# Column-group products, levels by halves and a fourth round: one large change to a three-stage audio kernel on TensorE

## What is computed

```python
h = einsum('bfh,kh->bfk', frames, D)                # DCT
# attention block, on layernorm(h)
q, k = exp(rmsnorm(xq @ Wq.T)), exp(rmsnorm(xk @ Wk.T));  v = xv_ @ Wv.T;  g = sigmoid(xg @ Wg.T)
A = lam * A + k v^T ;  z = lam * z + k              # per head, step by step over the frames
att = g * (q^T A) / (q . z) @ Wo.T
x = x + att
x = x + gelu(layernorm(x) @ W1.T) @ W2.T
h = h + x
# expert block, on layernorm(h)
x_attn = normed @ attn_w.T + attn_b + xf
y = gelu(x_attn @ fc1_w[e].T + fc1_b[e]) @ fc2_w[e].T + fc2_b[e]
h = h + gelu(y @ next_w.T + next_b)
```

## Time and profile before

| | us |
|---|---|
| median of 3 runs | 1223.17 |
| lowest and highest | 1221.0 and 1224.21 |
| the profiled execution | 1218.9 |
| its span, first to last instruction | 1217.1 |
| TensorE busy in it | 1138.9 (94%) |
| VectorE busy | 986.5 (81%) |
| ScalarE busy | 621.5 (51%) |
| GpSimd busy | 300.9 (25%) |

### The profile page before, as it was taken

How to read it: one execution, slowest core, us unless ns; L and a number is a source line. 1 busy time by engine, 2 the same in 40 slices (tenths; PEclk the granted TensorE clock), 3 DMA queues, 4 the chain that set the end, 5 groups by cost and what they waited for, 6 DMA issues and landing times.

```text
span 1217.1 us, 43497 instructions
## 1 busy us (share of the span) xinstructions
PE 1138.9 (94%) x17955; PEld 807.8 (66%) x17955; DVE 986.5 (81%) x3362; ACT 621.5 (51%) x1100; POOL 300.9 (25%) x174
## 2 busy tenths in 40 slices
PE   4799999999999999999999999999999999999997
PEld 4576676666767676766666667666676766667664
DVE  7878788797887979788796887979879797987962
ACT  3346446363554736446363554736446364554634
POOL 4123131221403223131311403223131221403211
PEclk8799999999999999999999999999999999999999
DMA  5321313222141312313222141312313222141210
GB/s 188 106 64 39 113 43 110 65 79 56 43 132 44 87 47 66 110 43 113 63 78 55 44 130 46 88 45 63 112 44 110 63 80 57 43 132 45 87 55 17
DMA packets 51492, 91.48 MB, mean 75 GB/s; under 512 B 9536, under 2 KB 26592, under 8 KB 51296
## 3 DMA queue, kind: packets, MB, share of 16 engines
q1 hardware_dynamic: 51296, 88.69, 24.1%
HBM read 19.50 MB, written 9.78 MB: 24 GB/s over the span
## 4 chain that ended last, share of the span: by engine, by line
PE 83%; DVE 9%; POOL 4%; issue 3%; ACT 2%; DVEq 0%; POOLq 0%
PE bank L1056 10%; PE bank L1049 9%; PE bank L1084 9%; PE bank L1078 8%; PE bank L919 8%; PE bank L914 7%; PE bank L1014 7%; PE bank L998 5%; PE bank L990 4%; PE bank L1033 4%; POOL nrm L391 3%; PE bank L1029 3%; PE bank L954 3%; PE bank L943 2%; PE bank L994 2%
## 5 line engine op out<-in xcount | busy, mean ns | idle before, releaser
L514 ACT ACTIVATE px<-bank 128x512 f32<-128x512 f32 (+1 forms) x128 | 72.8, 569 | 218.0 <-PE bank L998 152.9
L763 DVE COPY_PREDICATED px<-mask,bank 128x512 f32<-128x512 uint32 (+1 forms) x128 | 88.6, 692 | 79.6 <-issue 76.8
L1078 PE MATMUL bank<-xa,f1w 128*128 128x512 f32 (+1 forms) x256 | 124.7, 587 | 14.8 <-DVE qtok L704 13.0
L1056 PE MATMUL bank<-w,hid 128*128 128x128 f32 x1024 | 121.9, 277 | 17.2 <-ACT hid L533 17.2
L1056 PEld LDWEIGHTS bank<-w,hid 128*128 128x128 f32 x1024 | 116.7, 192 | 31.6 <-ACT hid L533 31.6
L1014 PEld LDWEIGHTS bank<-qx,ki 128*32 128x32 f32 x7680 | 89.6, 110 | 42.3 <-issue 33.9
L827 DVE TENSOR_TENSOR ki<-k,rp 128x96 f32<-128x96 f32 (+13 forms) x512 | 113.2, 295 | 0.6 <-ACT k L499 0.6
L397 POOL TENSOR_TENSOR ab<-af,heads 128x896 f32<-128x896 f32 x16 | 40.8, 2552 | 291.1 <-DVE af L755 291.1
L1049 PE MATMUL bank<-c,w 128*128 128x512 f32 (+1 forms) x256 | 111.4, 568 | 1.1 <-ACT c L527 0.9
L1084 PE MATMUL bank<-hid,f2w 128*128 128x512 f32 (+1 forms) x256 | 107.5, 563 | 0.0
L1014 PE MATMUL bank<-qx,ki 128*32 128x16 f32 x7680 | 99.2, 193 | 6.9 <-issue 6.6
(11 more groups left out here) (142 smaller groups left out, 2414.0 us busy)
## 6 DMA issues: line engine op xcount, KB each, us to landing
qx<-qq SPq DMA_DIRECT2D x256, 96.0 KB
hs<-hs SPq DMA_DIRECT2D x32, 532.0 KB, 4.4
v<-v_f SPq DMA_DIRECT2D x16, 512.0 KB, 3.9
gz<-gate_f SPq DMA_DIRECT2D x16, 512.0 KB, 4.7
xT<-in_xT SPq DMA_DIRECT2D x16, 468.5 KB, 4.0
f1w<-in_fc1T SPq DMA_DIRECT2D x16, 256.0 KB, 2.7
f2w<-g_dram SPq DMA_DIRECT2D x16, 256.0 KB, 3.0
out<-t_sum SPq DMA_DIRECT2D x16, 256.0 KB, 2.7
```

The costliest lines, as they stand in the source:

```text
L763: V.copy_predicated(px[c % 2][0:n, :, 0:n], mask[0:n, 0:n].rearrange("p (o m) -> p o m", o=1).to_broadcast([n, HEADS, n]), bank[DIAG][0:n, ...
L1056: last = mm(dst[:, P * i:P * i + P], hid[:, j, P * m:P * m + P], w2[:, j, :], start=(j == 0), stop=(j == 3))
L1078: mm(dst[:, 0:width[g]], f1w[:, P * j:P * j + P], xa[:, cols(g)], start=True, stop=True).then_inc(f1_ok, 1)
```

## The change

- **Products round the columns.** In `pairs_a` the 64-column product is two of 32 columns and comes first, then the two of L994, then the twelve of L990 with the window as the inner loop.
- **States by heads.** The state product of `scan` is four, one for each head's 32 columns.
- **Levels by halves.** `inside`, `between` and `qlev` run twice a batch on 512 frames. `ki`, `ko`, `kw` now hold one half; the second half's wait (`last_pairs`) is for `pairs_b(3)` of the same batch, the first half's for `pairs_b(7)` of the batch before.
- **The second norm on ScalarE.** `normed2` becomes one small VectorE instruction a half (`offset2`) and eight ACTIVATE a batch.
- **Fewer buffers cleared.** `qc` and `qq` no longer; of others only the frames beyond 938; `ki`, `ko`, `kw` just ahead of their first use in `inside` and `between` of batch 0. The first DMA of samples no longer waits for a clear.
- **Its own order.** LAST is 3, so 19 rounds. The DCT and the first transposes are stage 0; q, k, v up to `scan(3)`, `pairs_a(4)` and `attends(0)` stage 1; `pairs_b(4)` to the first half of the expert stage 2; the rest stage 3. Every engine's order and the bank table are new.

```diff
-LAST = 2
+LAST = 3
@@ def last_pairs
+        def last_pairs(eng, b, g):
+            if g:
+                eng.wait_ge(pb_ok, nth(b, TILES, TILES // 2))
+            else:
+                before(eng, pb_ok, b, TILES, TILES)
@@ spread
-                sp.wait_ge(ql_ok, nth(b, GROUPS, g + 1))
+                sp.wait_ge(ql_ok, nth(b, 2, g // 2 + 1))
@@ scalar
+            def normed2(b, g):
+                act.wait_ge(nb2_ok, nth(b, 2, g + 1))
+                before(act, n1T_ok, b, 2, g + 1)
+                for m in tiles(g):
+                    last = nc.scalar.activation(nl2[:, m, :], x2[:, m, :], ACT.Identity, scale=rr2[:, m:m + 1], bias=nb2[:, m:m + 1])
+                last.then_inc(nl2_ok, 1)
@@ vector
-            for tile in (k, qc, ga, gate_f, c1, xa):
-                V.memset(tile[:, :], 0.0)
-            for tile in (qq, ki, ko, kw):
-                last = V.memset(tile[:, :, :], 0.0)
+            for tile in (k, ga, gate_f, c1, xa):
+                last = V.memset(tile[:, T:PADT], 0.0)
...
-                dve.wait_ge(ek, nth(b, 2, g // 2 + 1))
-                last_use(dve, b, g)
+                dve.wait_ge(ek, nth(b, 2, g + 1))
+                last_pairs(dve, b, g)
...
             def inside(b, g):
+                if first(b) and g == 0:
+                    V.memset(ki[:, :, :], 0.0).then_inc(s_lev, 1)
+                    dve.wait_ge(s_lev, 1)
@@ pairs_a
-                for w in range(n):
-                    r, t0 = slice(WIN * w, WIN * w + WIN), P * o + WIN * w
-                    for j in range(1, NE):
...
+                if n == NW:
+                    t0 = Q64 + P // 2 * o
+                    for w in (0, 1):
+                        r = slice(WIN * w, WIN * w + WIN)
+                        mm(O[r, :, P // 2:P], kw[:, 1, k0 + WIN * w:k0 + WIN * w + WIN], x[:, :, t0:t0 + P // 2], start=True, stop=True)
                 for w in range(0, n, 2):
...
-                if n == NW:
-                    t0 = Q64 + P // 2 * o
-                    last = mm(O[0:P // 2, :, P // 2:P], kw[:, 1, k0:k0 + P // 2], x[:, :, t0:t0 + P // 2], start=True, stop=True)
+                for j in range(1, NE):
+                    for w in range(n):
@@ scan
                 if c:
-                    mm(S[:, s0:s0 + n], ab[:, c - 1, :], qc[:, P * c:P * c + n], start=True, stop=False, skip_group_check=True)
+                    for hd in range(HEADS):
+                        r = slice(HD * hd, HD * hd + HD)
+                        mm(S[r, s0:s0 + n], ab[:, c - 1, r], qc[:, P * c:P * c + n], start=True, stop=False, skip_group_check=True)
```

More of the change, by code:

```diff
@@ L415, in body @@
             def body(at):
+                if (b := at(2)) is not None:
+                    resid(b, 0); pow2(b, 1)
                 if (b := at(1)) is not None:
@@ L564, in body @@
+                if (b := at(1)) is not None:
+                    pxs(b, 2); attn_in(b); pxs(b, 3)
+                if (b := at(2)) is not None:
+                    xas(b, 1); fin(b, 0)
+                if (b := at(0)) is not None:
+                    hlT(b, 0)
                 if (b := at(2)) is not None:
                     gelu2(b, 1, 0)
-                if (b := at(1)) is not None:
-                    pxs(b, 3)
+                if (b := at(0)) is not None:
+                    hlT(b, 1)
@@ L570, in body @@
                 if (b := at(1)) is not None:
[L571 to L613 removed]
+                    pxs(b, 4)
             every_round(body)
@@ L838, in body @@
             def body(at):
+                if (b := at(1)) is not None:
+                    normed(b)
+                if (b := at(2)) is not None:
+                    gated(b, 0); inside(b, 1); attended(b, 0); stats2(b, 0); merge(b, 4)
+                if (b := at(1)) is not None:
+                    shifted(b)
+                if (b := at(2)) is not None:
+                    merge(b, 5); offset2(b, 0)
+                if (b := at(1)) is not None:
+                    mixes(b, 0)
+                if (b := at(3)) is not None:
+                    result(b, 0)
@@ new lines, in body @@
+                if (b := at(1)) is not None:
+                    tokens(b, 1, 0)
+                if (b := at(2)) is not None:
+                    stats3(b, 0)
+                if (b := at(1)) is not None:
+                    tokens(b, 1, 1)
+                if (b := at(2)) is not None:
+                    normed3(b, 0)
+                if (b := at(1)) is not None:
+                    qlev(b, 0); between(b, 0)
+                if (b := at(2)) is not None:
+                    hidden(b, 1)
@@ L843, in body @@
+                if (b := at(1)) is not None:
+                    inside(b, 0); denominators(b); from_start(b); chain(b); merge(b, 0)
+                if (b := at(0)) is not None:
+                    stats1(b, 1)
+                if (b := at(1)) is not None:
+                    gate(b, 0); merge(b, 1)
                 if (b := at(0)) is not None:
@@ L1092, in body @@
             def body(at):
+                if (b := at(3)) is not None:
+                    f1s(b, 1, 2); f1s(b, 1, 3); oTs(b, 0)
+                if (b := at(2)) is not None:
+                    pairs_b(b, 4); pairs_a(b, 5); pairs_b(b, 5); scan(b, 4); pairs_a(b, 6); pairs_b(b, 6); scan(b, 5)
+                if (b := at(3)) is not None:
+                    f2s(b, 1)
+                if (b := at(1)) is not None:
+                    qkv(b, "q", 0); qkv(b, "q", 1)
+                if (b := at(2)) is not None:
+                    n2Ts(b, 0); pairs_a(b, 7); pairs_b(b, 7)
@@ new lines, in body @@
+                if (b := at(1)) is not None:
+                    qkv(b, "k", 0)
+                if (b := at(3)) is not None:
+                    oTs(b, 1)
+                if (b := at(2)) is not None:
+                    w1s(b, 0, 0); scan(b, 6); scan(b, 7); w1s(b, 0, 1); attends(b, 1); w1s(b, 0, 2); w1s(b, 0, 3)
+                if (b := at(1)) is not None:
+                    qkv(b, "k", 1)
+                if (b := at(2)) is not None:
+                    w2s(b, 0); n2Ts(b, 1)
+                if (b := at(1)) is not None:
+                    qkTs(b, 0, 0)
```

361 lines of the change are left out of this document (171 added, 190 removed), and 10 rows, old and new, of the table USES.

## The result

The changed kernel takes 1186.7 us (median of 4 runs, 1186.2 to 1189.9) against 1223.7 for the kernel before on the same chip: a ratio of 0.970, 95% interval 0.966 to 0.974. The forecast was 1162, a gain of 61 us; 37 came.

What follows compares the result with a forecast made beforehand. TensorE's own work was taken as the bound: a round of 73.1 us less 2.8, 0.9 and 0.6 gives 68.8. With start and end the span is 1157 us; plus 4.3 for the median, 1162 was forecast, range 1130 to 1197.

Steps and rivals of the forecast that it cites:

- Products round the columns: pairs_a of tiles 0 to 6 on TensorE: 1.25 us becomes 0.85 each, a gain of 2.8 us a round.
- States by heads: State product of the seven scans on TensorE: 4.3 us becomes 3.4, gain 0.9 us a round, between 0.4 and 1.2.
- a sign of being wrong: In the profile after: pairs_a taking above 1.0 us from its first start to the next step's would show the prediction wrong.
- The prediction's 1.7 us by the page: Skill-page estimate: 64 weight loads in line would make pairs_a over 1.7 us and the change slower; prediction trusted the trace.
- Passages between widths: TensorE's other switches between 32-column and wider products: about as many as before, so worth nothing.
- Cover of ScalarE and VectorE: Their added work hides: ScalarE about 42 us, VectorE 56.7 busy a round; 5.4 us of TensorE work covers between(1) before pairs_a(4).
- the rival that ended slower: pairs_a(4) comes late through between(1), queries or merge(3), shifting VectorE's round: 6.2 us a round more, 1249 us; chance 0.05.
- VectorE as the bound: Rival: VectorE's round is 56.7 busy plus 12.4 waits, and a fifth more waiting gives 1193 us; chance 0.15.
- rotation brings nothing: Rival: pairs_a's L990 and L994 already overlap, so only width passages go: 70.2 us a round, 1182 us; chance 0.10.
- The waits: TensorE's waits in the new order, orders laid side by side: 2.4 us a round against 3.0, gain 0.6.
- the places I named: TensorE's waits: 0.4 behind w2s(0), 0.2 x_attn(0), 0.4 ahead of rTs, 0.9 pairs_b(1), 0.5 us pairs_b(2).
- theory F: Formed after the result: TensorE's instructions come in blocks of 256; short ones using one up in under some 3.5 us stall.

Runs made afterwards that it cites:

- e9: Kernel before with only the two TensorE edits (pairs_a round the columns, states by heads), in the old order, stages and banks; 1.006 of before.
- e5: Changed kernel with hidden(0) ahead of norms(1) in VectorE's order; 0.960 of the kernel before.
- e2: Changed kernel with every second product of pairs_b left out, so output isn't the reference's; 1099.4 us, 0.901 of before.
- e3: Changed kernel with 32 instead of 16 moving columns in each pairs_b product, as many instructions, other values than the reference's; 1201.0 us, 0.985 of before.
- e4: Changed kernel with the wide step f2s(1) moved on TensorE from behind scan(5) to between scan(4) and pairs_a(6); 1174.1 us, 0.962 of before.
- e11: Changed kernel with hidden(0) before norms(1), f2s(1) before pairs_a(6), half of f1s(0) behind pairs_b(0), dcts(1) before zts, f2s(0) halved around pairs_a(3); 1139.4 us.
- e7: Changed kernel with pairs_a as it was before, all else as changed; 0.976 of before.
- e8: Changed kernel with the state product of scan in one of 128 columns again, as before; 0.981 of before.
- e1: Changed kernel with another bank table: w1_10 to w1_13 in banks 4, 0, 3 and 1; 1.018 of before.
- e6: Changed kernel with f1s(0,2) and f1s(0,3) moved on TensorE from behind pairs_a(0) to behind pairs_b(0); 1194.6 us, 0.982 of before.

## Why the prediction was right, and where it was wrong

The time lies in the range and the sign is right, but the gain is 37 us of 61. TensorE's steps got shorter by 5.1 us a round (69.6 to 64.5 in the table) where 3.7 were forecast, and its waits grew by 2.7 where they were to shrink by 0.6. That the time stayed in the range is in part luck: with the steps as forecast and the waits as they came, 14 rounds would have been 3.3 us longer each, and 1162 + 46 is 1208, outside it.

**Products round the columns: right.** From the first start of L1048 to the next step it is 0.80 to 0.81 us in tiles 1, 2, 3 and 6 (553.70 to 554.50 above), where 0.85 was forecast and the earlier trace rows has 1.25; 2.5 us a round for 2.8. Tiles 0 and 4 have 0.95 and 0.93 with a 128-column step behind them, and tile 5 has 1.05, past the 1.0 that the prediction called a sign of being wrong. There it is a merge: `pairs_b(5)` starts 0.06 us behind the end of `merge(4)` in each of the 16 batches. VectorE, then TensorE:

```profile
569.71 0.73 DVE L786 COPY_PREDICATED px<-mask,bank 128x512 f32<-128x512 uint32 x1 [0.34 <-issue]
570.50 0.72 PE L1073 MATMUL bank<-qx,ki 128*32 128x16 f32 x62
```

So 0.25 us a round are a wait that the idle time hardly shows (0.04), because the last matmuls of `pairs_a(5)` are still listed as busy. The weight loads showed as little as I took from `pairs_b`. The prediction's 1.7 us by the page belongs to `pairs_b`, with its 64 weight loads; `pairs_a` has 32. By the Trainium skill's rule (TensorE: Matmul & The Clock Gate, Part 3, The mechanism) and the 27 ns a load of its section LDWEIGHTS they alone would take 0.86 us in line, an estimate from the page, with the matmuls on top. This trace has 0.80 for loads and matmuls together, and 0.54 for `pairs_b`, so it disagrees.

**States by heads: right, under-sized.** 1.6 us a round for 0.9, over my upper bound of 1.2. TensorE's timeline in the second run of short products:

```profile
571.04 0.28 PE L1091 MATMUL bank<-qc,ab 128*32 128x128 f32 x1
...
571.26 0.43 PE L1095 MATMUL bank<-px,v 128*32 128x128 f32 x8
571.48 0.40 PE L1048 MATMUL bank<-qx,kw 128*32 128x256 f32 x2
```

571.04 to 571.48 is 0.44 us for a scan where the earlier trace rows has 0.66.

**Passages between widths, valued at nothing: wrong, to the good, and the cause is open.** `f1s` lost 0.7 us a round and the other wide steps 0.8 (43.2 to 42.4), while `pairs_b` took 0.3 more: 1.2 us. It belongs to the new order, since e9, in the old one, has none of it. That it is passages is shown for none of it. The four products `f1s(1)` stood singly between transposes and short products, and lost 0.3. But `f1s(0)` lost 0.4, and in the kernel before it has 128-column work on both sides.

**Cover of ScalarE and VectorE: right.** VectorE is busy for 56.1 us of a round (56.7 forecast), ScalarE for 41.4 (42). TensorE never waits for a semaphore at `pairs_a(4)` in these rounds, so the rival that ended slower has no support, nor has VectorE as the bound. The time came nearest to that of "rotation brings nothing", 1182, but not its way: the rotation does what it should on TensorE, and its worth is lost in the waits.

**The waits: this is the step that failed.** 2.4 us a round were forecast and 5.7 came. Of the places I named, the one behind `w2s(0)` was right but hidden: e5 shows 0.45 us there for ScalarE's copy, for 0.4 forecast. At `pairs_b(1)` there are 0.19 us in the round above, and they stand in mid-step and have no name. What came is some 3.6 us a round without a name and 1.6 for `hidden(0)`. Two errors lie behind it.
- "That so many can be issued in that time is shown by `pairs_b`" took the pace of half a microsecond for one that lasts. The 15 us of unnamed waits in the kernel before were in its profile; I counted them among its 3.0 us a round and didn't ask what they were. Most of them stand in its runs of short products.
- The laying of the orders side by side followed semaphores between named steps, and let `hidden(0)` start as soon as its input was there. It did not follow the wait of the instruction ahead of it on VectorE, `norms(1)` on GpSimd.

**The sum.** 72.7 (the mean of 15 rounds; the one of the earlier trace rows had 73.1) - 2.5 - 1.6 - 1.2 + 2.7 of waits is 70.1, and 70.2 is measured for the 68.8 forecast. (In the forecast itself 1159 and 4.3 make 1163, not 1162.) From one `pairs_b(4)` to the next: the first comes at 79.5 (76.5 forecast), the next 68.3 later (63.4, of which about 2 are my boundary, since two products of `f1s` of the last stage stand ahead of it), then thirteen in 913.1 (894.4), one of 68.0 (66.1) and an end of 55.4 (57): 26.9 us over in all, 18.7 of them in the thirteen full rounds. q of batch 0 starts at 28.2 (28.7).

**What is shown and what isn't.** That the unnamed waits hang on how many instructions stand in how short a time, and not on merges, e2, e3, e4 and e11 show. That they are waits for a block rests on the packets' times and size and on the places of the waits, one and the same in every 256 instructions. Why so much is given back in e9 and e7, more than theory F gave by hand, is shown in part: e9 loses some 8 us to the clock, and e7 has none of the changed kernel's two falls, which are worth some 3. The rest is open. Levels by halves, the norm on ScalarE and the clears were not undone one by one; VectorE's spare 14 us a round says that the first two can bring nothing directly now.

## What to carry to other kernels

Count instructions, not only columns. Where a run of small matmuls takes up a block of 256, weight loads counted, in well under 3.3 us, making them shorter buys waits of the same length. The profile calls these "issue" in the middle of a step, and they can be told by their distance: a multiple of 256 instructions from one to the next. Put wide products between such runs (here two moves of about 2 us and one of 3.3 brought back 42 of 59 us of waits) and then shorten them, in that order. And when a wait ends with an engine's instruction, look at the one ahead of it in that engine's queue before touching buffers.

## What was not expected of the hardware

- An instruction packet of 16 KB holds 256 instructions, counted four times: 7 packets for 1792 instructions, 30 for 7680 (e2), and to the next whole packet 2 for 448 (e7) and 6 for 1344 (e8). Two packets are at least 3.2 us apart, so in the long run an instruction of TensorE costs some 13 ns at least, though `pairs_b` goes through 128 in 0.54 us.
- Where TensorE lacks instructions it stands still at the end of a block (470 of 507 unnamed waits), and only one block is brought ahead.
- The granted clock falls behind short waits: six of the nine falls of e1 follow its waits at `w1s(1)`, the longest of which is 1.5 us, the five of e9 follow waits of 1.8 to 2.3 us, and the eight of e6 a single one of 0.83 us. Not each such wait has a fall: e6 has 15 of them. In e1, behind 3.2 us of waits, a fall loses half as much again.
